# Attention's output and 20 feed-forward inputs turned by DMA, projection in three fp16 passes, new plan

## The chip, the cores and the metric

The kernel runs on one core of a Trainium2 chip. The metric is the device time of one execution in microseconds (us). The profile tells the busy time of TensorE (PE; PEld is its weight load), VectorE (DVE), ScalarE (ACT), GpSimd (POOL) and of the DMA queues, of which nearly all traffic goes through SyncE's (SP).

## What is computed

One sequence of 4096 tokens with 256 channels goes through four blocks, each added to its input after a normalization: a gated recurrence, a token-mixing feed-forward block, causal attention with 16 heads of 16 channels, and the feed-forward block again with the same weights.

```python
def _ln(x): return (x - mean(x)) / sqrt(var(x) + 1e-5)

def ffn(x, W_r, W_k, W_v, mu_r, mu_k):
    x_prev = concatenate([zeros, x[:, :-1]], axis=1)
    xr = mu_r * x + (1 - mu_r) * x_prev
    xk = mu_k * x + (1 - mu_k) * x_prev
    return sigmoid(xr @ W_r) * (square(relu(xk @ W_k)) @ W_v)

def attention(x):                       # q, k, v = x @ W.T + b, per head
    out = softmax(causal(q @ k.T / 4)) @ v
    return out @ Wo.T + bo

x = x + gated_recurrence(_ln(x))        # 4 gates, scan over tokens, own norm
x = x + ffn(_ln(x))
x = x + attention(_ln(x))
x = x + ffn(_ln(x))
```

## The kernel before

**Units and steps.** All but attention's inside is done in 16 units of 256 tokens. A unit's feed-forward block is called a layer: FIRST ahead of attention, LAST behind it, so 32 layers. Attention runs in 32 steps: for each chunk of 512 queries (8 chunks) the 16 heads in 4 groups, so step 4c+g is group g of chunk c, and it has 4(c+1) tiles of 128 keys. For each tile PE computes four heads' scores (L2130), ACT makes the exponentials (`probs`, L1523, L1534), POOL masks those on the diagonal (L1364), and PE multiplies them with the values (L2151, four heads beside each other in the columns). The maxima by which the exponentials are shifted are found beforehand: PE computes the same products once more (L2098) and DVE reduces each (`span_max`, L1828). That pass runs at most two steps ahead of the scores.

**Jobs beside attention.** Gates, q, k, v, the layers' products and the projection are PE jobs of two halves each. A product in fp32 takes the operand as it is. The gates, q, k and v of units 4 to 15 are done in parts: the operand is split on POOL into an fp16 upper part (`x1.hi`, `x3.hi`, L1199) and the rest (`x1.lo`, `x3.lo`, L1205), both are turned from token rows to channel rows by a DMA transpose (L1101), and PE sums three fp16 products (`channels_in_parts`, L1908). What is not turned by DMA is turned by PE, four 128x128 products with the identity (`to_channels`, L1882): the layer's input (`ffnT`, 32 times) and attention's output (`aT`, 16 times). ACT copies the result out of PSUM (`ffnT.copy` at L1437 with the last token's column at L1439; `aT.copy` at L1503). For the layer POOL then subtracts neighbours (`diff`, L1299) and mixes (L1309, L1312). The projection is `proj`, two halves of eight fp32 matmuls with `weights["ao"]`; in the profile each is 16 records at L1897.

**What sets the order.** A planner, `schedule()`, runs when the kernel is built. It knows what follows what (`followed()`), a cost for each operation (`COST`), and a table of weights with one number per attention step and kind of choice (`WORTH`). It writes one order for each engine and SP. On the chip each engine works its list off in that order and waits on semaphores. PE works in three shapes: `half` (two products of 64 rows beside each other: maxima and scores), `pv` (columns of 32: values and most jobs) and `full` (128x128: all transposes). One layer is in flight at a time, since `f_n`, `f_xr`, `f_xk` and `f_xT` exist once. Where PE finds too little to do at the start and the end, the plan puts in products with the identity (`warm`, L1936).

## Time and profile before

| | us |
|---|---|
| median of 3 runs | 1718.87 |
| lowest, highest | 1718.74, 1719.53 |
| the profiled execution | 1718.71 |
| its span, first to last instruction | 1717.0 |
| PE busy in the span | 1676.3 |
| DVE busy | 1501.6 |
| ACT busy | 1328.4 |
| POOL busy | 745.2 |

The steps aren't marked in the profile, but the score products are counted: steps 0 to 7 have 192 of the 2304, steps 0 to 19 have 960, steps 0 to 30 have 2176. So the first score product (133.8 us) starts step 0, the 193rd (304.3 us) step 8, the 961st (916.6 us) step 20, the 2177th (1625.6 us) step 31. The text uses the stretches between these points.

### The profile page before, as it was taken

The page shows a single profiled execution, that of the slowest core. Times are in us where ns is not written, and L with a number is a line of the kernel's source. Part 1 is how long each engine was busy: PE and PEld are TensorE (multiplying, and loading weights), DVE is VectorE, ACT ScalarE, POOL GpSimd, SP SyncE. Part 2 cuts the span into 40 slices and gives each one's busy share as a digit, 9 for nine tenths or more (in the row PEclk, how much of TensorE's full clock was granted, in tenths as well). Part 3 has the DMA queues.
Part 4 walks back from the last instruction along what each step waited for, and adds up shares of the span by engine and source line. Part 5 has one row for each costly group of instructions (what it writes and reads, how often), then busy time and mean ns, then how long its engine had stood idle before and what let it go on. Part 6 is the DMA issues. An engine that isn't in the chain of part 4 may idle for free.

```text
span 1717.0 us, 48248 instructions
## 1 busy us (share of the span) xinstructions
PE 1676.3 (98%) x19538; PEld 657.6 (38%) x19538; DVE 1501.6 (87%) x2874; ACT 1328.4 (77%) x2689; POOL 745.2 (43%) x1067
## 2 busy tenths in 40 slices
PE   8899999999999999999999999999999999999998
PEld 5665454444334443333443333332333222222224
DVE  6787887888999899999999999999999999999602
ACT  3346567767776778888768988888888989999894
POOL 3348877778654763736374124220412021200231
PEclk9999999999999999999999999999999999999999
DMA  4143122113103010121100010000020000000000
GB/s 115 45 88 62 35 57 52 33 29 65 42 14 62 19 37 13 33 43 24 33 15 25 14 25 19 18 12 2 14 43 6 6 14 6 14 2 2 2 14 19
DMA packets 83123, 50.18 MB, mean 29 GB/s; under 512 B 34901, under 2 KB 82901, under 8 KB 82901
## 3 DMA queue, kind: packets, MB, share of 16 engines
q1 hardware_dynamic: 80660, 46.04, 11.6%
q8 instruction: 154, 2.52, 0.6%
q10 hardware_dynamic: 2240, 1.05, 0.4%
q14 instruction: 69, 0.56, 0.1%
HBM read 24.00 MB, written 16.25 MB: 23 GB/s over the span
## 4 chain that ended last, share of the span: by engine, by line
PE 73%; DVE 16%; ACT 4%; issue 2%; POOL 2%; SPq 2%; DMA 1%; ACTq 0%; DVEq 0%; POOLq 0%
PE psum L2151 24%; PE psum L2098 14%; PE psum L2130 14%; DVE span_max L1828 12%; PE psum L1897 8%; PE psum L1889 4%; PE psum L1908 4%; ACT probs L1523 2%; PE psum L1882 1%; PE psum L2105 1%; PE psum L2160 1%; PE psum L1918 1%; DVE rows L1760 1%; DVE small L1670 1%; SPq L1019 0%
## 5 line engine op out<-in xcount | busy, mean ns | idle before, releaser
L1828 DVE TENSOR_REDUCE span_max<-psum 128x1 f32<-128x512 f32 (+1 forms) x2048 | 1244.7, 673 | 71.4 <-PE psum L2098 58.5
L1523 ACT ACTIVATE probs<-psum 128x512 f32<-128x512 f32 (+3 forms) x1788 | 874.4, 574 | 145.1 <-PE psum L2130 140.7
L2098 PE MATMUL psum<-k_stack,q_stack 48*128 48x512 f16 (+3 forms) x2304 | 549.5, 364 | 5.4 <-DVE span_max L1828 1.8
L2130 PE MATMUL psum<-q_stack,k_stack 50*128 50x512 f16 (+3 forms) x2304 | 525.2, 364 | 3.0 <-ACT probs L1534 0.9
L2151 PE MATMUL psum<-probs,v_aug 128*17 128x512 f32 (+3 forms) x3920 | 483.0, 564 | 1.9 <-ACT oT L1543 1.4
L2098 PEld LDWEIGHTS psum<-k_stack,q_stack 48*128 48x128 f16 x2304 | 160.6, 93 | 311.3 <-DVE span_max L1828 213.6
L2130 PEld LDWEIGHTS psum<-q_stack,k_stack 50*128 50x128 f16 x2304 | 147.8, 93 | 339.9 <-ACT probs L1523 180.3
L1364 POOL TENSOR_SCALAR_AFFINE_SELECT probs<-probs 128x512 f32<-128x512 f32 x115 | 73.4, 640 | 207.5 <-ACT probs L1523 198.6
L1523 ACT ACTIVATE w_gates<-psum 128x512 f32<-128x512 f32 (+1 forms) x296 | 145.9, 558 | 16.8 <-PE psum L2130 15.9
L2151 PEld LDWEIGHTS psum<-probs,v_aug 128*17 128x17 f32 x3920 | 66.5, 95 | 117.2 <-issue 101.6
L1357 POOL TENSOR_TENSOR rows<-rows 128x512 f32<-128x512 f32 x26 | 33.2, 1275 | 151.8 <-ACT rows L1460 151.8
L1534 ACT ACTIVATE probs<-psum 128x1024 f32<-128x1024 f32 (+2 forms) x86 | 83.9, 1078 | 6.8 <-PE psum L2130 6.1
L2105 PE MATMUL psum<-mask_keys,mask_rows 64*128 64x64 bf16 x1024 | 88.6, 189 | 0.0
L2105 PEld LDWEIGHTS psum<-mask_keys,mask_rows 64*128 64x128 bf16 x1024 | 75.8, 95 | 22.9
L2151 PE MATMUL psum<-w_gates,v_aug 128*17 128x512 f32 (+1 forms) x688 | 82.2, 550 | 0.1
L1316 POOL TENSOR_TENSOR rows<-rows 128x512 f32<-128x512 f32 x26 | 27.1, 1041 | 124.9 <-ACT rows L1449 124.9
L1908 PE MATMUL psum<-rows,w_gates 128*32 128x256 f16 x2304 | 77.9, 274 | 1.0 <-DMA rows<-rows 0.8
L1299 POOL TENSOR_TENSOR rows<-rows 128x512 f32<-128x512 f32 x26 | 27.1, 1042 | 110.4 <-ACT rows L1437 110.3
L1670 DVE BATCH_NORM_STATS2 small<-rows 128x6 f32<-128x256 f32 x160 | 59.3, 413 | 15.7 <-POOL rows L1335 12.3
L1889 PE MATMUL psum<-rows,w_k 128*32 128x256 f32 x1024 | 68.0, 383 | 4.0 <-DVE rows L1787 2.9
L1822 DVE TENSOR_REDUCE span_max<-psum 128x2 f32<-128x512 f32 (+1 forms) x128 | 65.8, 549 | 6.6 <-PE psum L2105 6.1
L1171 POOL TENSOR_SCALAR rows<-rows,small 128x256 f32<-128x256 f32 x124 | 68.1, 558 | 6.8
(175 smaller groups left out, 1715.6 us busy)
## 6 DMA issues: line engine op xcount, KB each, us to landing
q_stack<-q_parts SPq DMA_DIRECT2D x192, 32.0 KB, 1.9
k_stack<-k_parts SPq DMA_DIRECT2D x42, 128.0 KB, 4.7
rows<-in_x SPq DMA_DIRECT2D x16, 256.0 KB, 2.9
q_parts<-rows SPq DMA_DIRECT2D x32, 128.0 KB, 2.0
k_parts<-rows SPq DMA_DIRECT2D x32, 128.0 KB, 1.9
out<-rows SPq DMA_DIRECT2D x16, 256.0 KB, 2.1
x_rows<-rows SPq DMA_DIRECT2D x14, 256.0 KB, 2.2
rows<-x_rows SPq DMA_DIRECT2D x14, 256.0 KB, 2.7
```

The costliest lines, as they stand in the source:

```text
L1364: nc.gpsimd.affine_select(out=tri, in_=tri, compare_op=ALU.is_ge, fill=0.0, base=0, pattern=[[0, HG], [1, P]], channel_multiplier=-1).then ...
L1523: act.activation(probs_of(tile)[:, i, q0:], bank(b)[:, q0:], ACT.Exp, scale=SCALE / QK_SCALE).then_inc(exp_done, 1)
L1534: act.activation(probs_of(tile)[:, i:i + 2, q0:], psum[:, b * CHUNK:(b + 2) * CHUNK].rearrange("p (h q) -> p h q", h=2)[:, :, q0:], ACT.Ex ...
L1670: ins = nc.vector.bn_stats(stats[:, ln, j], src[:, j])
L1828: nc.vector.tensor_reduce(span_max[:, s % SPAN_RING, row:row + 1, k0 // SPAN:k0 // SPAN + 1], bank(b)[:, 0:k1 - k0], AX.X, ALU.max).then_i ...
L1889: ins = nc.tensor.matmul(bank_chan(b)[c:c + COLUMNS, e], w[:, k, e * P + c:e * P + c + COLUMNS], src[:, k], start=(k == 0), stop=(k == CT ...
L1897: ins = nc.tensor.matmul(bank_tok(b)[c:c + COLUMNS, j], src[:, k, j * P + c:j * P + c + COLUMNS], w[:, k], start=(k == 0), stop=(k == CT - 1))
L1908: ins = nc.tensor.matmul(bank_chan(b)[c:c + COLUMNS, e], w[:, y, k, e * P + c:e * P + c + COLUMNS], src[:, x, k], start=(k == 0 and n == 0 ...
L2098: ins = nc.tensor.matmul(bank(b)[:, at:at + k1 - k0], q_stack[row:row + SCORE_ROWS, s % Q_RING, v, qt * P:(qt + 1) * P], k_stack[row:row + ...
L2105: ins = nc.tensor.matmul(bank(b)[:, k:k + HALF], mask_rows[row:row + HALF, n], mask_keys[row:row + HALF], start=False, stop=(n == 1))
L2130: nc.tensor.matmul(bank(b)[:, q0:], k_stack[row:row + STACK, g * PAIRS + u, j * P:(j + 1) * P], q_stack[row:row + STACK, s % Q_RING, u, q0 ...
L2151: ins = nc.tensor.matmul(pv_bank[32 * h:32 * h + VW, q0:], v_aug[:, j, g * HG + h, :], probs_of(tile)[:, h, q0:], start=(j == 0), stop=(j ...
```

## The change

**Attention's output** of units 0 to 13 is no longer turned by PE. POOL splits it (`a.hi`, `a.lo`), SP turns both parts (`a.turn`, two DMA transposes), and the projection's halves are three fp16 passes of 24 matmuls. For that Wo is one of the weights in parts; it is loaded to scratch, its bound is found with the others', and v is held scaled, so that the first `v.copy` now waits for the scales. Units 14 and 15 use the old way, with Wo loaded once more over `weights["aq"]` and scaled by DVE (`load_ao`, `ao.scale`).

**The input of 20 layers** (FIRST of units 8 to 15, LAST of units 2 to 13) is split on POOL (`ff.hi`, `ff.lo`), turned by SP (`ff.turn`), and added up again by POOL (`ff.sum`), which also keeps the last column (`ff.last`). No PSUM bank, no PE transpose and no ACT copy is used there. All products of the layer stay fp32.

**Beside it** the ring of x rows shrinks from 3 to 2 buffers, whose room holds the split rows of attention's output; thus x of unit 2 is loaded only when unit 0 is through its own norm. `WORTH` has new numbers for most steps, and a few costs are new, so the whole plan is another one.

```diff
-X_ROWS = 3
+X_ROWS = 2
-PARTED = ("f", "i", "o", "s", "av", "aq", "ak")
+PARTED = ("f", "i", "o", "s", "av", "ao", "aq", "ak")
+TURNED_FROM = {FIRST: 8, LAST: 2}
+def turned(u, ln):
+    return u >= TURNED_FROM[ln] and not at_ends(u, ln)
...
-WORTH = {"max": (3001.09, 4221.2, 4221.2, 3001.09, 3001.09, 3001.09, 3001.09, 3001.09, 2554.7, 3001.09, 3001.09,
+WORTH = {"max": (1983.6, 4221.2, 5216.44, 3708.66, 3001.09, 2995.85, 3225.04, 3230.68, 2554.7, 3001.09, 3001.09,
...
+        if u < UNITS - LATE:
+            op(("a.hi", u), ("norm", (u // 2 + 1) * GROUPS - 1), ("a.turn", u - 1))
+            op(("a.lo", u), ("a.hi", u))
+            op(("a.turn", u), ("a.lo", u), ("p.x3", u - 1))
+            op(("proj", u, 0), ("a.turn", u), ("x2+bo", u), ("proj", u - 1, 1),
...
+            if turned(u, f):
+                op(("ff.hi", u, f), normalized(u, f))
+                op(("ff.lo", u, f), ("ff.hi", u, f))
+                op(("ff.turn", u, f), ("ff.lo", u, f))
+                op(("ff.sum", u, f), ("ff.turn", u, f), ("prev", u, f))
+                op(("ff.last", u, f), ("ff.sum", u, f))
...
-        op(("out", s), ("oT", s), *[("aT", 2 * c - n) for n in (1, 2) if g == 0])
+        op(("out", s), ("oT", s), *[("a.lo", 2 * c - n) for n in (1, 2) if g == 0])
...
+                elif op[0] == "ff.turn":
+                    sp.wait_ge(f_lo, BY_DMA[op[1:]] + 1)
+                    for j in range(UT):
+                        sp.dma_start_transpose(
...
+                elif op[0] == "a.lo":
+                    u = op[1]
+                    pool.wait_ge(a_hi, u + 1)
+                    nc.gpsimd.tensor_tensor(a_tokens[:, :, 1], attn[:, u % 2 * UT:(u % 2 + 1) * UT, :],
+                                            a_tokens[:, :, 0], ALU.subtract).then_inc(a_lo, 1)
...
+                elif op[0] == "ff.sum":
+                    v = LAYER[op[1:]]
+                    pool.wait_ge(f_turned, 16 * UT * (BY_DMA[op[1:]] + 1))
+                    pool.wait_ge(mixr_ready, v)
+                    nc.gpsimd.tensor_tensor(f_xT[:, :, 1:], f_parts[:, 0], f_parts[:, 1], ALU.add)\
+                        .then_inc(xT_ready, 1)
...
-                    ins = tokens_out(b, weights["ao"], c_columns(u), j)
+                    if u < UNITS - LATE:
+                        ins = tokens_in_parts(b, w_parts["ao"], aT_parts, j)
+                    else:
+                        ins = tokens_out(b, weights["aq"], c_columns(u), j)
```

**PE, a transpose of attention's output in the kernel before** (step 12). L2130 are scores, L2098 maxima, L2151 values, L1882 the transpose:

```order
L2098 MATMUL psum<-k_stack,q_stack 128x512
L2130 MATMUL psum<-q_stack,k_stack 128x512
L2098 MATMUL psum<-k_stack,q_stack 128x512
L1882 MATMUL psum<-ident,attn 128x128 x4
L2098 MATMUL psum<-k_stack,q_stack 128x512 x2
L2151 MATMUL psum<-probs,v_aug 17x512 x4
```

It stands between two pairs of 64-row products, so PE changes its shape before and behind it. No such row with `attn` is left for units 0 to 13 in the kernel after.

**PE, a projection in the kernel after** (step 9; L2249 scores, L2217 maxima, L2224 the mask, L2270 values, L2028 the projection in parts):

```order
L2270 MATMUL psum<-probs,v_aug 17x512 x4
L2028 MATMUL psum<-w_ao,rows 32x256 x24
L2249 MATMUL psum<-q_stack,k_stack 128x384 x2
L2217 MATMUL psum<-k_stack,q_stack 128x512
L2224 MATMUL psum<-mask_keys,mask_rows 128x64 x2
L2249 MATMUL psum<-q_stack,k_stack 128x384
```

The half stands behind values of the same shape; before, such a half was `L1897 MATMUL psum<-w_ao,rows 32x256 x8` in fp32.

**POOL, a layer's start in the kernel before** (unit 8, FIRST: L1290 keeps the last token, L1340 and L1347 split q and k, L1299 is `diff`, L1309 and L1312 mix):

```order
L1290 COPY rows<-small 128x2
L1347 TENSOR_TENSOR rows<-rows 128x512
L1340 TENSOR_SCALAR rows<-rows 128x512
L1330 TENSOR_TENSOR rows<-rows,bo_b 128x512
L1364 AFFINE_SELECT probs<-probs 128x4x128
L1347 TENSOR_TENSOR rows<-rows 128x512
L1299 TENSOR_TENSOR rows<-rows 128x512
L1309 TENSOR_SCALAR rows<-rows,small,cols 128x256 x2
```

**POOL, the same layer in the kernel after** (L1366 the last token, L1370 `ff.hi`, L1373 `ff.lo`, L1379 `ff.sum`, L1386 `ff.last`, L1396 `diff`):

```order
L1366 COPY rows<-small 128x2
L1370 TENSOR_SCALAR rows<-rows 128x2x256
L1373 TENSOR_TENSOR rows<-rows 128x2x256
...
L1326 TENSOR_TENSOR rows<-rows 128x512
L1379 TENSOR_TENSOR rows<-rows 128x2x256
L1337 TENSOR_SCALAR rows<-rows 128x512
L1341 TENSOR_SCALAR rows<-rows 128x512
L1386 TENSOR_SCALAR small<-rows 128x2
L1396 TENSOR_TENSOR rows<-rows 128x512
```

Four operations came in ahead of `diff`; eight others of other units stand between the split and the sum, while the rows are turned.

**SP around that layer in the kernel after** (L1147 `ff.turn`, L1141 `a.turn`, L1123 queries, L1133 shifts, L1097 x):

```order
L1147 DMA_TRANSPOSE rows<-rows 128x4x128 x2
L1123 DMA q_stack<-q_parts 16x2x512 x6
L1097 DMA rows<-in_x 128x2x256
L1123 DMA q_stack<-q_parts 16x2x512 x6
L1141 DMA_TRANSPOSE rows<-rows 128x4x128 x2
L1133 DMA q_stack<-shift_rows 2x512 x4
```

The transposes stand in the same queue as the loads of queries and shifts that the scores need.

Counted over the two orders of PE, with the stretches of the section above:

| in the order | steps up to 19, before / after | steps 20 to 30 | step 31 |
|---|---|---|---|
| transposes `aT` and `ffnT` | 30 / 10 | 13 / 0 | 5 / 4 |
| projection halves | 16 / 14 | 10 / 12 | 6 / 6 |
| layer product halves | 130 / 120 | 43 / 52 | 19 / 20 |
| gate halves in parts | 96 / 90 | 0 / 6 | 0 / 0 |
| maxima products (L2098 or its like) | 1068 / 1060 | 1108 / 1116 | 0 / 0 |
| value tiles | 237 / 238 | 304 / 306 | 35 / 32 |
| changes of PE's shape | 870 / 812 | 776 / 781 | 78 / 71 |

Ahead of the first score product stand 22 maxima products before and 12 after.

## Rows read from the trace of the kernel before

**Rows 1.** The page: busy time, share of the span, instructions of each engine.

```profile
PE 1676.3 (98%) x19538; PEld 657.6 (38%) x19538; DVE 1501.6 (87%) x2874; ACT 1328.4 (77%) x2689; POOL 745.2 (43%) x1067
```

**Rows 2.** Windows between the steps: stretch, its length, busy us (instructions) of each.

```profile
core 0: us, PE busy (x) PEld busy (x) DVE busy (x) ACT busy (x) POOL busy (x), PEclk, DMA share, GB/s
0.00:133.80 133.80, 120.36 (x1899) 82.64 (x1900) 98.61 (x271) 49.49 (x103) 51.13 (x93) 1.00 0.34 82
133.80:304.30 170.50, 163.69 (x2436) 81.17 (x2429) 137.86 (x294) 114.53 (x269) 136.13 (x199) 1.00 0.24 50
304.30:916.60 612.30, 605.46 (x7801) 247.22 (x7797) 569.05 (x1077) 465.17 (x979) 384.21 (x536) 1.00 0.14 33
916.60:1625.60 709.00, 704.24 (x6542) 215.95 (x6540) 681.93 (x1199) 632.86 (x1254) 149.56 (x209) 1.00 0.06 13
1625.60:1717.00 91.40, 82.57 (x883) 30.61 (x879) 14.15 (x36) 66.35 (x85) 24.20 (x33) 1.00 0.05 16
```

**Rows 3.** Chain of work: start us, us, what; PE's pieces by shape.

```profile
787.63 1.03 PE psum L1897 x16
...
791.38 2.08 PE psum L1908 x72
...
795.44 0.77 PE psum L1908 x24
...
797.73 0.59 PE psum L2160 x4
798.32 0.44 PE psum L1882 x4
...
1642.53 0.86 PE psum L2151 x8
1643.39 0.54 PE psum L2130 x4
1643.93 0.98 PE psum L2151 x8
...
1702.94 0.86 PE psum L1897 x16
```

**Rows 4.** Chain of work, from 1041 us on: the pieces of DVE.

```profile
1041.79 4.28 DVE span_max L1828 x7
...
1048.71 7.85 DVE span_max L1828 x13
```

**Rows 5.** Timeline of DVE at the last maxima, and ACT's window behind them.

```profile
1611.45 6.67 DVE L1828 TENSOR_REDUCE span_max<-psum 128x1 f32<-128x512 f32 x11
...
1630.00:1680.00 50.00, 48.75 (x444) 12.46 (x446) 1.69 (x6) 49.98 (x59) 18.27 (x23) 1.00 0.05 17
```

**Rows 6.** POOL's groups: form, count, busy us, mean ns of one.

```profile
L1321 POOL TENSOR_TENSOR rows<-rows 128x512 f32<-128x512 f32 x26 | 33.1, 1273 | 1.7
L1205 POOL TENSOR_TENSOR rows<-rows 128x512 f16<-128x512 f32 x24 | 28.8, 1201 | 0.4
L1199 POOL TENSOR_SCALAR rows<-rows 128x512 f16<-128x512 f32 x24 | 16.1, 670 | 9.5 <-DVE rows L1751 8.2 <-POOL rows L1270 0.2
L1290 POOL COPY rows<-small 128x2 f32<-128x2 f32 x32 | 7.1, 221 | 0.0
```

**Rows 7.** The DMA transposes at L1101: issue ns min/median/max, and time to landing.

```profile
L1101 SPq DMA_TRANSPOSE rows<-rows x48: 1189/1256/2470, 101.7 to 1213.8; - x48
...
DMA to landing us min/median/max: 2.4/2.5/6.6
```

**Rows 8.** Timelines around 390 us: a PE transpose of a layer, its copy, its `diff`.

```profile
389.50 0.66 PE L1882 MATMUL psum<-ident,rows 128*128 128x128 f32 x4
...
390.43 0.64 ACT L1437 ACTIVATE rows<-psum 128x512 f32<-128x512 f32 x1
...
392.10 1.05 POOL L1299 TENSOR_TENSOR rows<-rows 128x512 f32<-128x512 f32 x1
```

**Rows 9.** Keys of chunks 3 and 4: their load, DVE's first maxima, median landing.

```profile
394.53 3.37 SPq L1010 DMA_DIRECT2D k_stack<-k_parts  x6
...
407.51 3.08 DVE L1828 TENSOR_REDUCE span_max<-psum 128x1 f32<-128x512 f32 x5 [0.70 <-PE psum L2098]
...
533.35 3.47 SPq L1010 DMA_DIRECT2D k_stack<-k_parts  x6
...
575.55 1.95 DVE L1828 TENSOR_REDUCE span_max<-psum 128x1 f32<-128x512 f32 x3 [4.38 <-PE psum L2098]
...
k_stack<-k_parts SPq DMA_DIRECT2D x42, 128.0 KB, 4.7
```

**Rows 10.** Who waited for DVE's reduction L1828 (us, times).

```profile
  PEld psum L2098: 213.6, 404
```

**Rows 11.** Groups of PE's filling products, and of one weight's lower part on DVE.

```profile
L1936 PE MATMUL psum<-ident 128*128 128x128 f32 x210 | 27.0, 284 | 1.7 <-POOL ident L1133 1.7
...
L1644 DVE SCALAR_TENSOR_TENSOR w_aq<-v_aug,w_aq 128x512 f16<-128x512 f32 x1 | 0.7, 747 | 0.0
```

More of the change, by code:

```diff
@@ L297, in followed @@
     op(("ones.late",), *[(n, SPLIT_FROM - 1, 1) for n in ("f", "i", "s", "o", "q", "kk", "v")],
-       *[("w.lo", i) for i in range(len(PARTED))])
+       *[("w.lo", i) for i in range(len(PARTED))], ("bo.add",))
+    op(("load_ao",), ("q", UNITS - 1, 1))
+    op(("ao.scale",), ("load_ao",))
     op(("bo",), ("bound",))
@@ L366, in followed @@
         op(("v", u, 1), ("v", u, 0))
-        op(("v.copy", u), ("v", u, 1), *([("ones.late",)] if u == LATE_KEYS // UT else []))
+        op(("v.copy", u), ("v", u, 1), *([("ones.late",)] if u == LATE_KEYS // UT else []),
+           *([("g.scale",)] if not u else []))
         if u % 2:
@@ L389, in followed @@
             normalize(u, f)
-            op(("prev", u, f), normalized(u, f), ("ffnT.copy", u - 1, f), *([("consts",)] if not u else []))
-            op(("ffnT", u, f), normalized(u, f), *so_on("ffnT", u - 1, f))
-            op(("ffnT.copy", u, f), ("ffnT", u, f), ("prev", u, f), *so_on("ffnT.copy", u - 1, f))
-            op(("subtract" if at_ends(u, f) else "diff", u, f), ("ffnT.copy", u, f), ("prev", u, f))
+            op(("prev", u, f), normalized(u, f), ("ff.last" if turned(u - 1, f) else "ffnT.copy", u - 1, f),
+               *([("consts",)] if not u else []))
+            if turned(u, f):
[4 more added lines that the diff above has]
+                op(("ff.last", u, f), ("ff.sum", u, f))
+            else:
+                op(("ffnT", u, f), normalized(u, f), *so_on("ffnT", u - 1, f))
+                op(("ffnT.copy", u, f), ("ffnT", u, f), ("prev", u, f), *so_on("ffnT.copy", u - 1, f))
+            op(("subtract" if at_ends(u, f) else "diff", u, f),
+               ("ff.last" if turned(u, f) else "ffnT.copy", u, f), ("prev", u, f))
             mk, mr = ("mixk", "mixr") if at_ends(u, f) else ("p.mixk", "p.mixr")
@@ L983, in build, with unit_of @@
                 LAYER[op[1:]] = len(LAYER)
+        def unit_of(u, f):
+            return X_UNIT if turned(u, f) else 1.0
+        BY_PE = {k: n for n, k in enumerate(k for k in LAYER if not turned(*k))}
+        BY_DMA = {k: n for n, k in enumerate(k for k in LAYER if turned(*k))}
         COPIED = {}
@@ L1089, in _ @@
                                          shift_rows[i:i + MAX_ROWS]).then_inc(shift_placed[s % 2], 16)
+                elif op[0] == "a.turn":
+                    u = op[1]
+                    sp.wait_ge(a_lo, u + 1)
+                    if u:
+                        sp.wait_ge(x3_ready, u)
+                    for j in range(UT):
+                        sp.dma_start_transpose(
+                            out=aT_parts.rearrange("p r k t -> p (r k) t")[:, :, j * P:(j + 1) * P],
+                            in_=a_tokens[:, j].rearrange("p r d -> p (r d)")).then_inc(a_turned, 16)
+                elif op[0] == "ff.turn":
+                    sp.wait_ge(f_lo, BY_DMA[op[1:]] + 1)
+                    for j in range(UT):
+                        sp.dma_start_transpose(
+                            out=f_parts.rearrange("p r k t -> p (r k) t")[:, :, j * P:(j + 1) * P],
+                            in_=f_tokens[:, j].rearrange("p r d -> p (r d)")).then_inc(f_turned, 16)
+                elif op[0] == "load_ao":
+                    sp.wait_ge(full["q"], UNITS)
+                    sp.dma_start(weights["aq"][:], WoT.rearrange("(k p) e -> p k e", p=P)).then_inc(ao_loaded, 16)
                 elif op[0] in ("x1.turn", "x3.turn"):
@@ L1239, in _ @@
                             pool.wait_ge(x2_ready, v)
-                        normalize(f_n, a_stream[u % STREAMS] if ln == FIRST else c_stream, ln).then_inc(n_ready, 1)
+                        normalize(f_n, a_stream[u % STREAMS] if ln == FIRST else c_stream, ln,
+                                  unit=unit_of(u, ln)).then_inc(n_ready, 1)
                 elif op[0] == "x+beta" and op[1]:
@@ L1438, in _ @@
                     act.wait_ge(prev_ready, v + 1)
-                    act.activation(x_last[:, 0 if f == FIRST else 1], src[:, :, UNIT - 1:], ACT.Copy)\
-                        .then_inc(last_ready, 1)
+                    act.activation(x_last[:, 0 if f == FIRST else 1], src[:, :, UNIT - 1:], ACT.Copy,
+                                   scale=unit_of(u + 1, f)).then_inc(last_ready, 1)
                 elif op[0] == "r.tanh":
```

223 lines of the change are left out of this document (140 added, 83 removed), and 14 rows, old and new, of the table WORTH.

## The prediction, made before the changed kernel ran

> **What bounds the kernel now.** First the page's busy times [rows 1]: PE 98%, DVE 87%, ACT 77%, POOL 43%. PE's share alone can mislead, since two products of 64 rows beside each other count as much as one, so I read the windows between the steps next [rows 2]. From 133.8 to 916.6 us PE idles 6.8 + 6.8 = 13.6 us of 783, DVE 32.6 + 43.3 = 75.9 us: PE is the bound. From 916.6 to 1625.6 us PE idles 4.8 of 709 us and DVE only 27.1: both are nearly full. The chain of waits there has long pieces of DVE alone, 7 and 13 reductions one behind the other [rows 4], and the maxima products' weight loads waited 213.6 us for DVE's reductions in all [rows 10]. So in the late steps a PE that is relieved soon meets DVE. Behind the last maxima (1611.45 + 6.67 = 1618.1 us) ACT is the bound: busy 49.98 of 50 us [rows 5]. The span is therefore made of the time at which the last step's scores can start, 1625.6 us, and a rest of 91.4 us that PE's jobs hardly change.
>
> **Prices.** Four transposes take PE 0.44 us next to others of their shape (L1882 behind L2160) and 0.59 alone; a half in fp32 takes 0.86 behind work of its own shape and 1.00 to 1.03 alone, a half in parts 2.08 / 3 = 0.69 in a row of three and 0.77 alone; a value tile 0.86 behind its own shape, 0.98 else [rows 3]. So a change of shape costs 0.12 us, and 0.65 is a half in parts without one ((2.08 - 0.12) / 3).
>
> **PE, steps 0 to 19.** From the counts in the table of the change: 20 transposes fewer, 20 x 0.44 = 8.8; 58 changes fewer, 58 x 0.12 = 7.0; the projection 16 x 0.86 - 14 x 0.65 = 4.7. The new plan also leaves work for later: 10 layer halves, 10 x 0.86 = 8.6; 6 gate halves, 6 x 0.65 = 3.9; 8 maxima, some 0.11 each (0.54 for four, less 0.12, [rows 3]) 0.9; and it does one value tile more, 0.9. Sum: 33 us less. Nearly all of it lies in steps 8 to 19: up to step 7 only attention's units 0 and 1 are turned by DMA, and POOL gets new work there (below). I count 32, since DVE has to follow: its own work falls by 8 reductions, a scan and three units' statistics, about 9 us, so that it would idle 75.9 - 32 + 9 = 53 us of 751. It is at 96.2% behind 916.6 us (681.93 of 709) [rows 2], and 93% would be wanted here; so it can follow.
>
> **PE and DVE, steps 20 to 30.** PE: 13 transposes fewer, 5.7, and the projection 10 x 0.86 - 12 x 0.65 = 0.8; but 9 layer halves (7.7), 6 gate halves (3.9), 2 value tiles (1.7), 8 maxima (0.9) and 5 changes (0.6) more: 14.8 - 6.5 = 8 us more. DVE: the 8 reductions, at 7.85 / 13 = 0.60 [rows 4], 4.8, and what came over of scan and statistics: 9 us more, with 27 us idle before. Both say the same: 9 us longer.
>
> **Step 31.** PE loses a transpose, 3 value tiles and 7 changes, some 3.5 us, but ACT sets the pace and its exponentials stay; half a us. The last 30 us, units 14 and 15, are as before.
>
> **The new waits.** POOL gets for each of 20 layers `ff.hi` 0.67, `ff.lo` 1.20, `ff.sum` 1.27 (from the sum of two fp32 rows; its fp16 inputs stand in no row, so 1.20 to 1.30) and `ff.last` 0.22, and for 14 units `a.hi` and `a.lo` 1.87 [rows 6]: 20 x 3.36 + 14 x 1.87 = 93 us on an engine that idles 972 us. On SP 34 pairs of transposes at 1.26 us each are 85 us in its queue. A layer's path from the normalized rows to `diff` was 392.10 - 389.50 = 2.6 us [rows 8]; now it is 0.67 + 1.20 + 1.26 + 2.5 + 1.27 + 0.22 = 7.1 us [rows 6, 7]: 4.5 us longer. Other work covers it, and most keys have room: those of chunk 4 are issued from 533.35 and first used at 575.55 us; but those of chunk 3 are issued from 394.53 to 397.9 and used at 407.51, with DVE waiting [rows 9]. `out` of each chunk's first step now waits for `a.lo` on POOL instead of a PE transpose; behind it stand `recip` and `norm` on DVE, and the reductions behind these. The second `a.hi` of a chunk waits for the first one's turn, which waits in SP behind `p.x3`. A step is 612.3 / 12 = 51 us long on average in steps 8 to 19, so there is room; I give all of these waits 2 us together, from 0 to 8. The splitting of Wo (one more upper and lower part, 0.7 us on ACT and DVE each [rows 11]), two more products for its bound and x of unit 2, loaded later, fall in the first 133.8 us, where PE idles 13.4 us and has most of its 27 us of filling products [rows 11]; the first scores stand behind ten maxima products fewer in the new order. I take 0, from -4 to +5.
>
> **The sum.** -32 + 9 - 0.5 + 2 = -21.5 us. The profiled execution took 1718.71 us at a span of 1717.0, 0.16 below the median of 1718.87. So 1718.87 - 21.5 = 1697.4 us, 1.25% faster; the span about 1695.5.
>
> **A rule that speaks against it.** A layer's four transposes take PE 0.59 us and the two DMAs that take their place need 3.8 us from issue to landing [rows 3, 7]. The Trainium skill, "VectorE: DVE Perf Modes", section "Rules for kernel authors", says to transpose 128x128 on TensorE if PSUM will do as the target, and by DMA otherwise; PSUM did here. By that rule the layer's latency decides and the change loses (third rival). The row agrees on the latency; but the rule counts no engine's load, and PE's 0.59 us is the scarcer good as long as the layers are covered.
>
> **Rivals.**
> *DVE takes most of it.* DVE idles where its products are late, and its reductions are not even. If in steps 8 to 19 it stays as full as it was, 569.05 of 612.3 us, or 93%, with 9 us less work, that stretch shrinks by 9 / 0.93 = 10 us, not 32; then 9 longer behind it would make nothing, but there the maxima that are late go on as now, and 27 idle us take half of the 9. -10 + 4.5 - 0.5 = -6, 1713 us; halfway to the forecast it is 1705. For it: [rows 4, 10]. Against: DVE is at 96% as soon as the plan gives it products.
> *More than forecast.* The new table of weights also fills better: PE's idle 13.6 us and half of DVE's waits in steps 8 to 19 go, and the start is 4 us shorter. -21.5 - 4 - 6 = -31.5: 1687 us.
> *The layers' path becomes the bound, and the kernel slower.* The place is the keys: FIRST of units 2c and 2c + 1 must be through, and one layer is in flight at a time. Each turned layer is 4.5 us longer. Between the keys of chunks 3 and 7, some 16 turned layers lie: 72 us if none is covered. The room at chunk 4 is 575.55 - 536.8 - 4.7 (median landing of a load of keys [rows 9]) = 34 us. It costs time from 34 us uncovered on and is a loss from 34 + 21.5 = 55 us, three quarters of the 72; with all of them uncovered the end is 72 - 34 = 38 us later, less the 21.5 won: 1735 us.
> *POOL becomes the bound ahead of step 8.* It is busy 136 of 170.5 us there, 80% [rows 2], and the new order puts some 19 us more in: `a.hi`, `a.lo` for two units (3.7), a layer's and a normalization's work that stood later. If it can't be fuller than 80% the stretch grows by 19 / 0.8 = 23 us, which is the whole gain: 1720 us. At 90% it costs 2 us. This decides from 80%.
> *It doesn't do what it says.* The transposes of 34 groups and the 28 halves are gone from PE's order for certain; that PE's time follows is open only as far as above.
>
> **Chances.** Forecast (1691 to 1702) 0.50; DVE takes a good part (1702 to 1714) 0.26; more than forecast (1684 to 1691) 0.14; POOL or the layers' path, partly or wholly (1714 to 1735) 0.10, of which 0.06 end above 1722. About 0.2%, 3.4 us, is what a measurement of this kernel can tell from no change: faster than 1715.4 us 0.91, within 0.2% 0.03, slower than 1722.3 us 0.06. The range leaves out 0.07 at the lower end and 0.11 at the upper: 1686 to 1711 us.
>
> **What would show it.** Right: step 8's first score product (the 193rd) at 300 to 308 us, step 20's (961st) at 880 to 890 and step 31's (2177th) at 1600 to 1607 us; PE busy near 1650 us; DVE idle in steps 8 to 19 down from 43 to 20 to 30 us; the part behind step 31 91 us within 1. DVE's share: step 20's later than 895 us with DVE idle 40 us there. POOL's: step 8's later than 315 us, POOL over 88% busy ahead of it. The layers': weight loads of maxima waiting for a DMA of `k_stack`. The prediction is wrong in its main step if step 20 comes at its old time although PE has 30 us less to do.

## The result, and the profile after

The changed kernel took 1705.26 us (median of 4 runs, 1703.14 to 1706.85), the kernel before 1718.80 us beside it: 0.992 of the time, 95% interval 0.9903 to 0.9938. 13.5 us were won where 21.5 were forecast. Its profiled execution took 1704.0 us at a span of 1702.2 us.

The page's busy times, to be read against [rows 1]:

```profile
PE 1652.0 (97%) x19619; PEld 649.9 (38%) x19619; DVE 1499.0 (88%) x2880; ACT 1316.0 (77%) x2638; POOL 828.6 (49%) x1175
```

PE has 24 us less to do, as forecast (near 1650 us), and POOL 83 more, where 93 were forecast. Windows between the same score products as in [rows 2], with the same columns (the third figure from the end is the granted clock):

```profile
0.00:140.70 140.70, 120.92 (x1874) 87.43 (x1874) 95.06 (x270) 49.82 (x104) 55.33 (x97) 0.98 0.31 74
140.70:315.10 174.40, 170.38 (x2651) 87.22 (x2651) 148.41 (x319) 118.26 (x276) 152.56 (x223) 0.99 0.28 56
315.10:894.50 579.40, 568.30 (x7283) 225.29 (x7279) 549.17 (x1033) 447.14 (x927) 368.56 (x513) 1.00 0.19 40
894.50:1611.80 717.30, 711.17 (x6938) 219.17 (x6936) 692.26 (x1225) 634.91 (x1250) 223.99 (x307) 1.00 0.09 20
1611.80:1702.20 90.40, 81.27 (x883) 30.79 (x883) 14.14 (x36) 65.82 (x84) 28.18 (x39) 0.99 0.07 19
```

| stretch | before | after | difference | forecast |
|---|---|---|---|---|
| ahead of the first scores | 133.8 | 140.7 | +6.9 | 0 (-4 to +5) |
| steps 0 to 7 | 170.5 | 174.4 | +3.9 | in the next row |
| steps 8 to 19 | 612.3 | 579.4 | -32.9 | -32, and +2 for waits |
| steps 20 to 30 | 709.0 | 717.3 | +8.3 | +9 |
| step 31 | 91.4 | 90.4 | -1.0 | -0.5 |

So the plan's large pieces came as forecast, and what is missing was lost ahead of 315 us. There the granted clock, 1.00 in all of [rows 2], reads 0.98 and 0.99. Narrower windows of the changed kernel, and under them two of the same of the kernel before:

```profile
98.00:101.00 3.00, 2.99 (x51) 1.70 (x40) 1.62 (x5) 1.60 (x3) 0.00 (x0) 1.00 0.72 151
101.00:104.00 3.00, 0.22 (x6) 0.00 (x0) 2.65 (x8) 0.00 (x0) 0.90 (x2) 0.97 1.18 129
104.00:108.00 4.00, 3.37 (x80) 3.00 (x84) 2.07 (x10) 0.00 (x0) 0.00 (x0) 0.60 1.13 155
104.00:106.00 2.00, 1.37 (x28) 1.20 (x32) 2.00 (x10) 0.00 (x0) 0.00 (x0) 0.50 1.15 116
123.00:126.00 3.00, 1.85 (x16) 1.15 (x17) 3.00 (x5) 0.00 (x0) 2.67 (x2) 1.00 0.52 127
128.00:132.00 4.00, 4.00 (x58) 1.98 (x54) 4.00 (x9) 0.28 (x1) 0.00 (x0) 0.61 0.02 4
158.00:162.00 4.00, 3.69 (x43) 1.99 (x42) 4.00 (x9) 3.14 (x7) 3.82 (x7) 0.98 0.98 138
162.00:166.00 4.00, 4.00 (x36) 1.99 (x40) 3.08 (x12) 1.61 (x5) 3.66 (x8) 0.59 1.33 133
389.00:392.00 3.00, 0.06 (x4) 0.00 (x0) 1.15 (x5) 0.59 (x2) 0.00 (x0) 1.00 1.33 178
392.00:396.00 4.00, 3.84 (x90) 2.61 (x94) 1.61 (x3) 2.00 (x5) 2.89 (x5) 1.00 0.79 120
```

```profile
101.00:104.00 3.00, 2.41 (x25) 1.82 (x17) 2.56 (x9) 0.84 (x2) 0.90 (x2) 1.00 1.15 129
104.00:108.00 4.00, 3.17 (x51) 2.18 (x53) 2.66 (x9) 0.60 (x1) 0.89 (x2) 1.00 1.40 176
```

Between 101 and 104 us PE was busy for 0.22 of 3 us; behind that the clock stood at 0.50 for some 3 us, which is 1.2 GHz in place of 2.4. It fell for as long at 128 and at 162 us, where PE had been less idle or hardly idle. It did not fall at 389 us, where PE idled nearly as long as at 101 us (3.10 against 3.40 us). One minus the granted clock, times the length of its window, is an estimate of what such a stretch costs a busy PE: 1.7 us each, 5.1 us for the three. The timeline of the first one (start, us, engine, line, idle time before it and its releaser):

```profile
97.48 2.62 SPq L1164 DMA_TRANSPOSE rows<-rows  x2
...
98.81 0.34 ACTq L1055 DMA_DIRECT2D k_stack<-k_parts  x1
...
99.18 2.68 ACTq L1055 DMA_DIRECT2D k_stack<-k_parts  x5
...
104.63 5.14 PE L2018 MATMUL psum<-rows,w_gates 128*32 128x256 f16 x135 [3.40 <-DMA rows<-rows]
```

The chain of waits tells the landing of the second transpose (start, us, what):

```profile
98.84 5.65 DMA rows<-rows
```

Unit 4's gate input is being turned when ACT issues the six loads of chunk 0's keys; the second transpose lands after 5.65 us, PE idles 3.40 us and goes on at 1.2 GHz. In the kernel before the same transposes took as long (the 6.6 us of [rows 7]), but PE came to these gates only at 112 us. The Trainium skill, "TensorE: Matmul & The Clock Gate", section "HAM oscillation — how this bites in real kernels", tells this of a PE that waits for a DMA before each batch of products: it goes on at the lower clock. The trace agrees at 104 us. It doesn't at 392 us, where PE waited 3.10 us for a transpose and went on at 2.4 GHz, and at 162 us it doesn't tell the cause, since PE was busy 3.69 of the 4 us ahead.

### The profile page after: what moved, and what is told of

It is laid out like the page before. It is cut to its first block, busy times and chain, and to the rows that moved or that the text cites. A ratio compares the mean times of both kernels' runs of the same rounds, so it can differ in the third digit from the quotient of the medians.

```text
span 1702.2 us, 48542 instructions
## 1 busy us (share of the span) xinstructions
PE 1652.0 (97%) x19619; PEld 649.9 (38%) x19619; DVE 1499.0 (88%) x2880; ACT 1316.0 (77%) x2638; POOL 828.6 (49%) x1175
## 4 chain that ended last, share of the span: by engine, by line
PE 63%; DVE 21%; ACT 6%; POOL 4%; issue 3%; SPq 2%; DMA 2%; ACTq 0%; POOLq 0%; DVEq 0%
PE psum L2270 20%; DVE span_max L1938 17%; PE psum L2217 12%; PE psum L2249 11%; PE psum L2007 6%; PE psum L1999 5%; PE psum L2018 4%; ACT probs L1623 3%; PE psum L2028 1%; DMA rows<-rows 1%; PE psum L2224 1%; DVE span_max L1932 1%; PE psum L2279 1%; ACT probs L1634 1%; DVE small L1780 1%
## 5 line engine op out<-in xcount | busy, mean ns | idle before, releaser
L1623 ACT ACTIVATE probs<-psum 128x512 f32<-128x512 f32 (+3 forms) x1806 | 886.5, 570 | 161.2 <-PE psum L2249 157.5
L2217 PE MATMUL psum<-k_stack,q_stack 48*128 48x512 f16 (+3 forms) x2304 | 557.6, 364 | 7.5 <-DVE span_max L1938 4.4
L2249 PE MATMUL psum<-q_stack,k_stack 50*128 50x512 f16 (+3 forms) x2304 | 542.4, 364 | 4.3 <-DMA q_stack<-shift_rows 1.0
L2270 PE MATMUL psum<-probs,v_aug 128*17 128x512 f32 (+3 forms) x3936 | 484.7, 565 | 1.2 <-ACT oT L1643 1.0
L2217 PEld LDWEIGHTS psum<-k_stack,q_stack 48*128 48x128 f16 x2304 | 162.8, 93 | 330.6 <-DVE span_max L1938 240.1
L2249 PEld LDWEIGHTS psum<-q_stack,k_stack 50*128 50x128 f16 x2304 | 150.8, 93 | 322.6 <-ACT probs L1623 179.3
L1623 ACT ACTIVATE w_gates<-psum 128x512 f32<-128x512 f32 (+1 forms) x280 | 139.7, 559 | 18.0 <-PE psum L2249 17.6
L2270 PEld LDWEIGHTS psum<-probs,v_aug 128*17 128x17 f32 x3936 | 67.4, 95 | 124.8 <-issue 110.5
L2224 PE MATMUL psum<-mask_keys,mask_rows 64*128 64x64 bf16 x1024 | 87.8, 189 | 0.0
L2224 PEld LDWEIGHTS psum<-mask_keys,mask_rows 64*128 64x128 bf16 x1024 | 75.1, 96 | 25.1 <-issue 0.3
L1634 ACT ACTIVATE probs<-psum 128x1024 f32<-128x1024 f32 (+2 forms) x81 | 79.5, 1119 | 5.5 <-PE psum L2249 5.1
L2270 PE MATMUL psum<-w_gates,v_aug 128*17 128x512 f32 (+1 forms) x672 | 80.7, 552 | 0.0
L1449 POOL TENSOR_SCALAR rows<-rows 128x512 f32<-128x512 f32 x26 | 16.1, 619 | 124.8 <-ACT rows L1541 124.8
L2018 PEld LDWEIGHTS psum<-rows,w_gates 128*32 128x32 f16 x2304 | 58.4, 97 | 29.5 <-issue 21.0
L1454 POOL TENSOR_TENSOR rows<-rows 128x512 f32<-128x512 f32 x26 | 33.1, 1273 | 74.8 <-ACT rows L1558 74.8
```

The source lines that it names most:

```text
L1623: act.activation(probs_of(tile)[:, i, q0:], bank(b)[:, q0:], ACT.Exp, scale=SCALE / QK_SCALE).then_inc(exp_done, 1)
L1634: act.activation(probs_of(tile)[:, i:i + 2, q0:], psum[:, b * CHUNK:(b + 2) * CHUNK].rearrange("p (h q) -> p h q", h=2)[:, :, q0:], ACT.Ex ...
L2018: ins = nc.tensor.matmul(bank_chan(b)[c:c + COLUMNS, e], w[:, y, k, e * P + c:e * P + c + COLUMNS], src[:, x, k], start=(k == 0 and n == 0 ...
L2217: ins = nc.tensor.matmul(bank(b)[:, at:at + k1 - k0], q_stack[row:row + SCORE_ROWS, s % Q_RING, v, qt * P:(qt + 1) * P], k_stack[row:row + ...
L2224: ins = nc.tensor.matmul(bank(b)[:, k:k + HALF], mask_rows[row:row + HALF, n], mask_keys[row:row + HALF], start=False, stop=(n == 1))
L2249: nc.tensor.matmul(bank(b)[:, q0:], k_stack[row:row + STACK, g * PAIRS + u, j * P:(j + 1) * P], q_stack[row:row + STACK, s % Q_RING, u, q0 ...
```

## The experiments

Twelve kernels ran, in three groups beside the kernel before, which took 1720.8, 1721.7 and 1719.9 us there (median clock of its runs 0.998, 0.998, 0.999). The last column is the loss by the clock in the profiled run, as worked out above. A kernel's span at full clock, where the text gives one over all its runs, is the mean of span times granted clock; for the changed kernel it is 1695.7 us over its ten runs.

| kernel | median us | against before (95%) | clock of its runs | step 8 / 20 / 31 starts, span | lost |
|---|---|---|---|---|---|
| changed, again | 1703.86 | 0.9908 (0.9889-0.9927) | 0.992-0.997 | 312.2 / 892.9 / 1611.0, 1701.5 | 5.1 |
| keys behind the turn | 1702.86 | 0.9888 (0.9868-0.9907) | 0.992-0.998 | 314.2 / 893.6 / 1610.6, 1701.0 | 8.5 |
| own buffer for unit 2 | 1706.38 | 0.9905 (0.9888-0.9922) | 0.993-0.997 | 319.0 / 898.0 / 1615.3, 1705.7 | 11.9 |
| both | 1701.90 | 0.9881 (0.9861-0.9901) | 0.993-0.997 | 312.5 / 893.2 / 1610.2, 1700.7 | 8.5 |
| filled | 1699.79 | 0.9872 (0.9852-0.9893) | 0.997-0.999 | 310.9 / 890.4 / 1608.0, 1698.4 | 1.7 |
| filled, turn first | 1702.02 | 0.9892 (0.9878-0.9907) | 0.996-0.999 | 309.8 / 891.3 / 1608.4, 1698.8 | 1.7 |
| transposes put back | 1722.98 | 1.0008 (0.9996-1.0020) | 0.994-0.997 | 313.8 / 900.8 / 1625.7, 1717.0 | 5.1 |
| two reductions more | 1722.57 | 1.0013 (1.0004-1.0023) | 0.992-0.997 | 317.5 / 907.7 / 1630.5, 1720.9 | 10.2 |
| old weights | 1793.30 | 1.0417 (1.0400-1.0434) | 0.970-0.974 | 341.5 / 984.2 / 1702.6, 1790.7 | 47 |
| old weights behind step 19 | 1713.80 | 0.9951 (0.9932-0.9970) | 0.988-0.995 | 322.1 / 901.4 / 1628.3, 1719.6 | 20 |
| before, new weights | 1825.50 | 1.0610 (1.0595-1.0626) | 0.971-0.972 | 343.9 / 1024.4 / 1733.7, 1824.0 | 51 |
| new plan, unit 2 early | 1780.92 | 1.0344 (1.0327-1.0361) | 0.978-0.981 | 327.1 / 946.9 / 1690.0, 1779.4 | 36 |

### The start: keys behind the turn, a buffer for unit 2

```diff
                 if op[0] == "act.load_k":
+                    act.wait_ge(x1_turned, 16 * UT)
                     load_keys(act, op[1])
```

> One wait is added to the changed kernel: ACT issues the load of chunk 0's keys only after the DMA transposes of unit 4's gate input have landed. In the changed kernel the two ran beside each other, the transposes landed late, PE idled 3.4 us up to 104.6 us, and its granted clock then read 0.50 (1.2 GHz) for some 3 us, so unit 4's gates took 5.1 us for 135 products. Theory: this collision is a piece of its own of the 6.9 us by which the first score product comes late, and it carries through to the end. Then PE does not idle at 101 to 105 us, the clock stays at 1.00 there, the first score product comes at 136 to 137.5 us instead of 140.7, and the time is 1705.1 - 4 = 1701 us. Rival: what the first scores wait for is something else (the plan's order of the first maxima, which stand behind the keys), then the first score product stays at 140 to 141 us or comes later since the keys land later, and the time stays at 1704 to 1706 us.

The first score product came at 136.6 us, and the 3.40 us of idle PE were gone. But the clock fell four times besides, at 37, 78, 157 to 164 (twice as long) and 379 us, and took 8.5 us. With the clock's loss taken off, the spans are 1692.5 against 1697.1 us of the changed kernel (1696.4 in its second profile): the collision cost 4 us, as the theory says. Over all runs the span at full clock is 1692.1 against 1695.7 us, so 3.6. The forecast time of 1701 us wasn't reached: in the medians the collision shows as 1 us, in the ratios as 0.2%, less than their intervals, since the clock fell elsewhere.

```diff
+def x_buffer(u):
+    return u if u < 3 else (u + 1) % 2
...
+        a_x.append(rows_[:, after_x - ROW:after_x].rearrange("p (t d) -> p t d", t=UT))
```

> The changed kernel, with the order of every engine unchanged, but x of unit 2 gets a buffer of its own (the rows that later hold the split of attention's output) and is loaded at the start, and units 3 and 4 take the buffers of units 0 and 1. Theory: x of unit 2, which in the changed kernel can only be loaded when unit 0 is through, is what makes PE idle and fill between 20 and 40 us; unit 2's gates then come some 8 us earlier (at 34 instead of 43 us), the filling products stay and cost PE 19 us as before, and the first score product comes at 134 to 137 us instead of 140.7; the time is 1705.1 - 5 = 1700 us. Rival: each engine's order was written for the late x, so other work of that order (the scales, the bounds, unit 1) holds unit 2 where it was: first score product at 139 to 141 us and 1703 to 1706 us.

> Both edits together: x of unit 2 in a buffer of its own, and chunk 0's keys loaded behind unit 4's transposes. If the two losses are separate pieces, the gains add up: first score product at 131 to 134 us, 1705.1 - 9 = 1696 us. If they are one (unit 2 in time means that the key load and unit 4's transposes no longer meet), the result is that of the better of the two alone, 1700 us.

The theory fell. Unit 2's gates started at 45.48 us with x in time:

```profile
45.48 2.80 PE L2011 MATMUL psum<-rows,v_aug 128*32 128x256 f32 x48 [0.78 <-ACT rows L1493]
```

Each engine works off an order that was written for the late x, and holds unit 2 to its place. Both edits together won what the first one won, or a little less: 1692.9 us at full clock over all runs, with the buffer alone 1694.5. The first scores, less the clock's loss ahead of them, came at 137.3 and 136.1 us in the two profiles of the changed kernel, 133.2 with the keys behind the turn, 135.3 with the buffer, 133.0 with both; 133.8 before. So the start's 6.9 us are the collision (3 to 4) and the clock (3.4).

### The clock

> The changed kernel itself once more, so that its clock can be read on the same chip as the others. In three profiles of its near relatives the granted clock fell to 0.50 (1.2 GHz) in 3 to 6 short stretches, all ahead of 400 us, and each lost 1.7 us. Theory: that is what the changed kernel has that the kernel before had not in its first profiles: the mean clock is 0.994 to 0.997 here, and time lies 1.7 us higher for every 0.001 of it, so 1704 to 1708 us. Rival: the low clock was of the relatives alone; then it reads 0.999 to 1.000 and about 1699 us.

So it was, and two runs were lower still: 0.992 to 0.997, with a median at the lower edge of the theory's range (1703.86 us). The runs lie near a line: at 0.997 four of the runs with transposes put back took 1719.0 to 1721.9 us, at 0.994 three took 1724.1 to 1727.0, so 5 us for 0.003. The kernel before has falls too in these later runs, but fewer: 1716.9 to 1719.2 us at 1.000 (three runs), 1726.1 and 1728.1 at 0.995. That makes the gap wider here than in the first comparison: 17.8 us in the medians (0.9908), where it was 13.5 (0.992); at full clock it is some 21 us in both.

```diff
+        for op, n in ((("yT", 1, 0), 16), (("ffnT", 0, 2, 1), 7), (("x1T", 2, 0), 3), (("f", 2, 0, 0), 6),
...
+            ORDER.insert(ORDER.index(op), ("warm", n))
...
+                        if (name, u) == ("f", 10):
+                            for n in range(12):
+                                nc.tensor.transpose(bank(b)[:, n % 4 * P:(n % 4 + 1) * P], ident[:], ident[:])
```

> The wait for chunk 0's keys behind unit 4's transposes (as tried before: 1702.9 us), and 77 more filling products of PE with the identity, 0.11 us each, at ten places ahead of the first scores where PE idled 0.4 to 2.0 us, and 12 at each of two later places where PE waits for a DMA transpose (unit 4's q at 233 us, unit 10's gates at 391 us). Results stay the same. Theory: the stretches at 1.2 GHz follow stretches in which PE had idled; filled, those at 37, 78, 104, 120 to 130, 238 and 390 us stay away, only some at 150 to 170 and at 378 us are left (PE was busy ahead of these), the mean clock rises from 0.995 to 0.998 or more, and the time falls by 4 to 6 us against the version without filling, to 1698 us. Rival: the filling products only take PE's time and the clock goes by something else, it stays at 0.995 and the time is 1703 to 1707 us.

The theory held for the clock: 0.999 in three runs and 0.997 in one. The time is 1699.79 us, none of its runs (1697.64 to 1701.67) above the lowest of the changed kernel beside it (1703.22). Against the version without filling it is 3.1 us less in the medians, not 4 to 6, and the intervals of the two ratios overlap, so this gain isn't clear of noise. Its windows, to be read against those of the changed kernel:

```profile
101.00:104.00 3.00, 3.00 (x96) 2.61 (x92) 2.65 (x7) 0.00 (x0) 0.90 (x2) 1.00 0.39 94
104.00:108.00 4.00, 4.00 (x128) 3.75 (x117) 2.12 (x10) 2.70 (x6) 1.44 (x3) 1.00 1.14 191
...
162.00:166.00 4.00, 2.91 (x44) 1.37 (x45) 2.89 (x6) 1.65 (x5) 3.92 (x5) 1.00 0.27 51
384.00:388.00 4.00, 1.58 (x33) 1.30 (x34) 0.51 (x3) 0.00 (x0) 0.00 (x0) 0.98 1.40 160
388.00:392.00 4.00, 4.00 (x66) 2.22 (x60) 1.25 (x2) 1.63 (x4) 3.56 (x7) 0.60 0.60 70
```

The only fall left, in this profile, follows a place where PE still idled though 12 products had been put in, 2.42 us at 385 to 387 us for unit 10's turn beside chunk 3's keys. The filling products aren't free: with the clock's loss taken off the span is 1696.7 (1695.4 over all runs, against 1692.1 without them), so the 4 us that the keys' wait had won are gone. They trade a sure 3 to 4 us for 3 to 7 uncertain ones. It has the lowest median of this study all the same.

```diff
+        ORDER.remove(("x1.turn", 10))
+        ORDER.insert(ORDER.index(("load_k", 3)), ("x1.turn", 10))
```

> The filled version with one exchange on SP: unit 10's DMA transposes are issued ahead of the load of chunk 3's keys instead of behind it. In the profiles so far PE idled 1.5 to 3.1 us there (up to 387 to 392 us), since the transposes landed 5.7 us after their issue beside the keys' six DMAs, and the clock mostly fell to 1.2 GHz behind it for another 1.7 us. Theory: the transposes land after 2.5 us, PE goes on, the clock stays up; 2.5 + 1.7 = 4 us less, 1699.8 - 4 = 1696 us, clock 0.999 to 1.000. The keys land 3 us later, at 390 us, and are first used at 405 us, so that they cost nothing. Rival: the transposes wait in the queue for their split rows of POOL, and the keys and queries behind them come late; then PE waits elsewhere and the time stays at 1699 to 1701 us.

A miss: 1702.02 us. PE no longer waited for the turn, but behind it the keys and the next transfer in the queue, x2 for unit 2's last block, were issued later: x2 at 383.74 us in place of 382.15, and POOL could add to it at 390.09 in place of 388.11. The timeline there (L1433 adds bo to x2, L1787 are the statistics, L2230 the maxima products):

```profile
379.56 4.07 SPq L1061 DMA_DIRECT2D k_stack<-k_parts  x6
383.74 0.38 SPq L1177 DMA_DIRECT2D rows<-x_rows  x1
```

```profile
390.09 1.27 POOL L1433 TENSOR_TENSOR rows<-rows,bo_b 128x512 f32<-128x512 f32 x1 [7.76 <-DMA rows<-x_rows]
...
396.38 0.75 DVE L1787 BATCH_NORM_STATS2 small<-rows 128x6 f32<-128x256 f32 x2 [4.73 <-POOL rows L1332]
...
397.79 0.39 PE L2230 MATMUL psum<-k_stack,q_stack 48*128 48x512 f16 x1 [3.25 <-DVE span_max L1945]
```

POOL waited 7.76 us for x2, DVE 4.73 us for POOL, with reductions queued behind the statistics, and PE 3.25 us for DVE; the clock fell again at 399 us. POOL had waited for x2 in the filled version too, but 4.76 us. The wait went round three engines and came back to PE. At full clock the two versions are level over all runs (1695.3 and 1695.4 us); the 2 us between their medians are the clock's (0.997 and 0.999 in the median).

### What PE's and DVE's time is worth

```diff
                     if j == 0:
                         claim(b, t_ready, LAYER[u, f] + 1)
+                        if turned(u, f):
+                            for k in range(CT):
+                                for n in range(UT):
+                                    nc.tensor.transpose(bank(b)[:, (k * UT + n) * P:(k * UT + n + 1) * P], ident[:], ident[:])
```

> The changed kernel with PE's four transposes put back as dead work: at each of the 20 turned layers and 14 turned outputs of attention PE transposes the identity four times into the bank that the next product overwrites. All DMA transposes, the order and the results stay. It measures what PE's transposes alone cost, with nobody waiting for them: 10 layers and 5 outputs lie in steps 8 to 19, 9 and 6 in steps 20 to 30, 2 in steps 0 to 7, 2 in step 31. Theory (PE is the bound in steps 8 to 19 as in the forecast): 0.59 to 0.71 us each incl. the change of shape, so steps 8 to 19 get 9 to 10 us longer, steps 20 to 30 as much (PE idles only 6 of 717 us there), 21 us in all: 1726 us. Rival (DVE sets the pace): PE takes the transposes in time in which it waits for DVE's reductions, steps 8 to 19 grow by under 4 us and the whole by under 10: 1715 us.

Steps 8 to 19 and 20 to 30, first with the transposes, then the changed kernel's second profile (one fall of the clock in steps 8 to 19 of each):

```profile
313.80:900.80 587.00, 578.62 (x7345) 230.18 (x7343) 550.67 (x1033) 447.03 (x927) 368.44 (x513) 1.00 0.19 40
900.80:1625.70 724.90, 718.90 (x6996) 223.94 (x6992) 693.89 (x1225) 634.99 (x1249) 223.41 (x307) 1.00 0.09 20
```

```profile
312.20:892.90 580.70, 569.84 (x7283) 226.28 (x7279) 549.33 (x1033) 447.10 (x927) 368.22 (x513) 1.00 0.19 40
892.90:1611.00 718.10, 711.64 (x6936) 219.17 (x6932) 693.52 (x1225) 635.09 (x1249) 223.76 (x308) 1.00 0.10 20
```

+6.3 and +6.8 us for 15 places each, 15.5 us in the span for all 34: 0.46 us a place. Over all runs at full clock it is 17.9 us (1713.6 against 1695.7, ten runs each), 0.53 a place. The bare price of four transposes is 0.44 [rows 3]. Beside it the transposes brought 45 changes of PE's shape at the 34 places, which at 0.12 us would be 5.4 us more; 0.5 us of them show in the profile, some 3 over all runs. The rival (under 4 us in steps 8 to 19, under 10 in all) is refuted, and the theory's 9 to 10, 9 to 10 and 21 us were not reached either. PE's busy time grew by 8.8 us in steps 8 to 19 and the stretch by 6.3; behind step 20 it is 7.3 and 6.8, in the whole span 17.3 and 15.5. So nearly all of PE's time counts, 90% in the whole, and less of it in steps 8 to 19.

```diff
+                        if row in (0, HG) and k0 == 0 and 8 <= s < 28:
+                            nc.vector.tensor_reduce(span_max[:, s % SPAN_RING, row:row + 1, 7:8],
+                                                    bank(b)[:, 0:SPAN], AX.X, ALU.max)
```

> The changed kernel with two dead reductions of 0.62 us more on DVE for each of steps 8 to 27 (40 in all; each reads a bank of maxima once more and writes to a place that nobody reads). The maxima pass runs about two steps ahead, so some 24 of them fall between steps 8 and 20, 12 behind, 4 ahead. Theory: besides PE, DVE is at its limit too, in the late steps above all; PE's products wait for its reductions, so behind step 20 each shows with its full 0.6 us (7 us more), in steps 8 to 19, where DVE idles 30 us, with about half (7 us more): 1705 + 15 = 1720 us. Rival: PE alone is the bound, as the transposes put back with their whole 0.4 to 0.5 us suggest, and DVE's idle time takes them: under 5 us, 1710 us.

```profile
317.50:907.70 590.20, 576.11 (x7283) 226.55 (x7280) 562.45 (x1056) 448.16 (x927) 367.35 (x512) 0.99 0.19 39
907.70:1630.50 722.80, 714.77 (x6938) 220.06 (x6934) 699.19 (x1237) 635.73 (x1249) 223.94 (x307) 1.00 0.09 20
```

Behind step 20, 12 reductions lengthened the stretch by 4.7 us, 0.39 each; in steps 8 to 19, 23 by 9.5, of which two more falls of the clock are 3.4, so 6.1 or 0.27 each. The price of one is 0.62. So DVE's time counts for 44 to 63% (59% over all runs at full clock: 1710.3 against 1695.7 us for 40 reductions), beside PE's at some 90%: nearer to the theory than to the rival. 5.1 of the 19.4 us by which the span grew came by the clock.

### What the weights do

> The changed kernel with the planner's weights of the kernel before. It tells what the moved transposes give and what the new weights give. Theory: the gain is that of the moved transposes and the projection, and the weights only place it; the time is between 1702 and 1712 us, with step 20 later than 894.5 us (20 gate halves and 6 layer halves more stand ahead of it) and step 31 as much nearer. Rival: without the new weights new waits of POOL and DVE lie open, and the time is 1717 us or more, so that the weights are most of the gain.

> The changed kernel with the new weights for steps 0 to 19 and the old ones for steps 20 to 31. With the old ones everywhere the loss lay ahead of step 20 (step 8 at 341.5 in place of 312.2 us, step 20 at 984.2 in place of 892.9 us), and behind it the stretches were as long as before (718.4 and 88.2 us). Theory: the weights decide where PE has many kinds of jobs to choose from, up to step 19, and hardly behind; the time is 1703 to 1712 us. Rival: behind step 20 an order that was not fitted loses as much per step; 11 of 32 steps would be 30 us, 1735 us.

> The kernel before with the planner's weights of the changed kernel. The changed kernel with the old weights took 1793 us, 88 us more than with its own. Theory: a table of weights fits one set of jobs and costs only, and the code before loses with the new one much as the new code with the old one: 1760 to 1800 us, with a granted clock under 0.99. Rival: the new weights are better by themselves, and the kernel before takes 1705 to 1719 us with them; then the gain would be theirs and not that of the moved transposes.

> x of unit 2 in a buffer of its own, and now the planner knows it, so that all engines' orders are new: unit 2 stands early in them. With the old order the free buffer alone won nothing (unit 2's gates at 45 us, first score product at 142.1). Theory: the late x of unit 2 costs because the order is written for it; in the new order unit 2's gates come at 32 to 38 us and the first score product, with 30 maxima products ahead of it in place of 12, at 136 to 140 us, step 8 at 306 to 310 us, and the end goes with it, 1700 us. Rival: the weights belong to the other plan, and the new order loses elsewhere what it wins here, 1705 to 1715 us; by the order it has 16 more gate halves in steps 8 to 19 and 8 layer halves fewer in step 31, so step 20 would come at 900 us or later.

The first of these fell to its rival. The second ended 1.8 us above its theory's range and far from the rival. The third took 25 us more than the upper end of its theory, and the fourth 66 us more than the upper end of its rival. The changed kernel with the old weights is 89 us slower than with its own, the kernel before with the new ones 106. Steps 8 to 19 of these two:

```profile
341.50:984.20 642.70, 621.46 (x7782) 248.53 (x7782) 554.94 (x1050) 452.41 (x945) 407.57 (x572) 0.96 0.18 39
```

```profile
343.90:1024.40 680.50, 659.87 (x7974) 262.33 (x7971) 557.23 (x1060) 469.71 (x988) 406.62 (x575) 0.95 0.14 33
```

642.7 in place of 580.7 us. The counts explain 14 of the 62 (20 gate halves at 0.65 and 6 layer halves at 0.86 more, a few products less), the clock 24 (0.04 of 642.7 less the 1.7 us of the other), PE's idle time 10 (21.2 against 10.9), and 14 are left open. Weights of the old kernel behind step 19 alone cost 10 us in the median (5 at full clock over all runs), and 8.8 in steps 20 to 30 of the profile (726.9 against 718.1), not the 30 us of the rival. With room for unit 2 known to the planner, 77 us are lost. A table of weights fits one set of jobs and costs, and no other in these four tries; "the weights only place it" was wrong, and so was the gain from a new plan with unit 2 early. No run fits a table anew for the kernel before, so how much a longer fit alone would win there is open.

## Why the prediction came out as it did

*Steps 0 to 19, -32 us.* The stretches up to step 20 shrank by 22.1 us; 5.1 were taken by the clock and 6.5 by PE's idle time for two late turns (3.40 at 104 us, 3.10 at 392 us). Without these it is 33.7. "Nearly all of it lies in steps 8 to 19" held (-32.9). One term of that sum is confirmed in part at most: 58 changes of shape at 0.12 us, 7.0 us, while 45 changes put back with the transposes cost between 0.5 and 3 us. What else gave as much is open; that the sum still fits is in this part luck.

*Steps 20 to 30, +9, and step 31, -0.5.* +8.3 and -1.0. DVE idled 25.0 of the 717 us of steps 20 to 30.

*The start, 0 from -4 to +5.* This step failed: +6.9 us. The reasons were not those weighed (Wo's splitting, the late x, fewer maxima), but a transfer that met another one and the clock behind it. The table of counts leaves out the maxima products of 128 columns; with them 30 stand ahead of the first score product before and 16 after. [rows 7] had the 6.6 us landing, which in the trace is that of the transpose issued at 101.7 us; that PE would come to these gates 8 us earlier, and so meet it uncovered, could have been read from the new order.

*The new waits, +2, 0 to 8.* PE waited for turned gate inputs and q's inputs:

```profile
  PE psum L2018: 7.4, 3
DMA to landing us min/median/max: 2.4/2.5/5.8
```

7.4 us in three waits, near the upper end; two of them beside a load of keys. None was for a layer or for attention's output. A layer's path, forecast at 7.1 us, was 7.1 in four of the 20 layers and up to 21.8 where POOL's order put other work between. POOL idled 30.5 us for the turned rows; no wait of PE was for them. POOL's sum of two fp16 halves took 1157 ns, not 1270:

```profile
L1379 POOL TENSOR_TENSOR rows<-rows 128x512 f32<-128x512 f16 x20 | 23.1, 1157 | 30.5 <-DMA rows<-rows 30.5
```

*What had no step at all: the clock.* It read 1.00 in every row of the kernel before, and the sum took that over. It cost 5.1 us in both profiles of the changed kernel, and 7.2 on average in its first four runs (clocks 0.997, 0.995, 0.997, 0.994: 0.00425 x 1702). With it taken off, the span is 1697.1 and 1696.4 us against the forecast 1695.5. So the mechanism and the main terms were right, and of the 7.9 us between forecast and result the clock has nearly all. The 1.6 us left in the first profile are a balance: waits took 6.5 us where 2 were given, the stretches up to step 20 won 1.7 more than their 32 and those behind it cost 1.2 less than their 8.5.

*The signs.* The prediction had named windows for being right: step 8 at 300 to 308 us, step 20 at 880 to 890, step 31 at 1600 to 1607. All three came later, at 315.1, 894.5 and 1611.8 us; at full clock they are 310.0, 889.4 and 1606.7, so that step 8 alone stays out. The part behind step 31 (90.4) and PE's busy time were inside.

*The rivals.* DVE idled 30.2 us in steps 8 to 19 (43.3 before), at the end of the forecast 20 to 30: it followed. POOL's sign was nearly met in the first profile, step 8 at 315.1 us and POOL 87% busy ahead (88 was asked); but in the second it came at 312.2, and PE is busy 168.9 of 172.7 us there: the stretch holds more of PE's own jobs (5 gate halves, 2 of the projection, 18 maxima products). No run relieves POOL there, so a small share of its own isn't excluded. The layers' path and the rule for transposes on PE did not decide: 15.5 to 17.9 of the some 20 us won at full clock are the transposes.

*What the argument lacked.* The waits were bounded by a layer's room on average. The runs with other weights have the same jobs and the same room, and lose 77 to 106 us. The forecast held because this order is fitted, and its counts alone could not have told that from an order that is not.
